# Which engine takes the third of the probabilities' low halves: DVE (before) or POOL (after)

## The reference, cut to what matters

```
h = tok(x)                                  # 16 images, 256 rows (tokens) of 256
h = h + attn(layernorm(h), Wq, bq, ...)     # 16 heads of 16, causal
h = h + ffn(layernorm(h), router, experts)  # 16 experts

attn: q, k, v = x Wq + bq, x Wk + bk, x Wv + bv
      scores  = (q k^T + mask) / sqrt(16)
      out     = softmax(scores) v           # for each image and head
```

## The kernel before, in words

| engine | steps at their places |
|---|---|
| PE | each place: the scores for the row maxima (lines 440 to 449), then the transposed scores for the exponential (463 to 472). 0, 1: product v. 3, 4, 6, 7, 9, 10, 0, 1: `times_v`. 3: transposes for xT (534), which wait for v_sum, since they use the same bank. 10: router product (525) |
| ACT | each place: exp n, n = (place + 2) mod 12, and then the rounding of probs n - 1. 2: negmax_hi. 3: first part of v (667). 4: xT_hi (649). 6: second part of v, hn2T. 8, 10: q_hi, k_hi. 11: router hidden |
| POOL | each place but 1, 4, 7, 10: low half n, n = (place + 1) mod 12. 4: v_rest (273) and the sum into hacc (280). 7: last part of v (276). 8: two times rstd (239, 241), for LN1 and LN2 |
| DVE | each place: the reduce to the row maximum (709, 713). 2, 5, 8, 11: `outputs`, then low half n = place (878). 2: v_sum (891). 5: xT_lo (863). 9: q_lo, second step of LN2 (756). 11: k_lo, then the normalised rows hn2 (769, two instructions). 1: hn1 (769, two instructions) |

## Time and profile before

### The profile page before, as it was taken

The page is one execution under the profiler, slowest core; times in us unless marked ns, Lnnn a source line. Parts: engine busy times, 40 slices in busy tenths (PEclk is TensorE's granted clock), DMA queues, the critical chain, the costliest instruction groups (busy, mean ns, idle before and its releaser), DMA issues.

```text
span 1197.5 us, 18952 instructions
## 1 busy us (share of the span) xinstructions
PE 939.6 (78%) x6870; PEld 806.0 (67%) x6870; DVE 734.1 (61%) x1598; ACT 575.2 (48%) x1065; POOL 678.9 (57%) x582
## 2 busy tenths in 40 slices
PE   0002147988888888877539999999999999999996
PEld 0002136767766776755318888888888888888885
DVE  6988846788888888875555345344444434544441
ACT  0000012777777877878414445444544544454442
POOL 2486041566656665656333567656656765665654
PEclk9999568899999999998759999999999999999999
DMA  8211749788688768811313545545445454555433
GB/s 209 90 54 67 158 124 141 122 127 136 130 143 134 131 126 146 137 42 37 125 55 69 107 112 86 109 110 119 97 107 114 85 106 112 109 106 108 83 53 36
DMA packets 105949, 127.59 MB, mean 107 GB/s; under 512 B 12288, under 2 KB 92160, under 8 KB 104832
## 3 DMA queue, kind: packets, MB, share of 16 engines
q1 hardware_dynamic: 81280, 92.81, 36.1%
q0 software_dynamic: 24576, 33.57, 17.2%
HBM read 79.67 MB, written 46.14 MB: 105 GB/s over the span
## 4 chain that ended last, share of the span: by engine, by line
PE 48%; DVE 2%; POOL 1%; issue 1%; ACT 0%; DMA 0%; POOLq 0%; ACTq 0%
PE y_ps L1120 15%; PE gate_ps L1106 15%; PE value_ps L1106 15%; PE xT_ps L1087 2%; DVE top_index L1260 1%; DVE top L1254 1%; DVE work L1262 0%; PE gate_ps L1129 0%; POOL out L1062 0%; POOL x_rows L1051 0%; DMA x_rows<-normed_scratch,slot_row 0%; ACT L1188 0%; ACT router_hidden L1188 0%; ACT xg_hi L1153 0%; DVE L L1252 0%
## 5 line engine op out<-in xcount | busy, mean ns | idle before, releaser
L1062 POOL DMA_INDIRECT out<-y_rows,slot_row x128 | 203.3, 1588 | 189.3 <-ACT y_rows L1166 159.9
L1229 DVE TENSOR_TENSOR hidden<-silu_g,value_ps 128x512 f32<-128x512 f32 x128 | 88.0, 688 | 306.5 <-PE value_ps L1106 171.5
L248 POOL TENSOR_TENSOR probs_k<-probs_full,probs_k 128x512 f16<-128x512 f32 x128 | 157.4, 1231 | 133.9 <-ACT probs_k L622 130.0
L1174 ACT ACTIVATE silu_g<-gate_ps 128x512 f32<-128x512 f32 x128 | 76.6, 598 | 276.7 <-PE gate_ps L1106 276.7
L1051 POOL DMA_INDIRECT x_rows<-normed_scratch,slot_row x128 | 149.6, 1169 | 56.4 <-issue 38.7
L615 ACT ACTIVATE probs_full<-scoresT_ps,log 128x512 f32<-128x512 f32 x192 | 132.4, 690 | 89.0 <-PE scoresT_ps L465 45.9
L1120 PE MATMUL y_ps<-w_hi,hidden_lo 128*128 128x256 f32 x512 | 144.9, 283 | 0.0
L1120 PE MATMUL y_ps<-w_lo,hidden_hi 128*128 128x256 f32 x512 | 144.9, 283 | 0.0
L1120 PE MATMUL y_ps<-w_hi,hidden_hi 128*128 128x256 f32 x512 | 144.7, 283 | 0.0
L622 ACT ACTIVATE probs_k<-probs_full 128x512 f16<-128x512 f32 x192 | 120.3, 627 | 0.0
L1106 PE MATMUL gate_ps<-xg_hi,w_hi 128*128 128x512 f32 x256 | 103.5, 404 | 2.1 <-ACT xg_hi L1153 2.1
(11 more groups left out here) (201 smaller groups left out, 2329.1 us busy)
## 6 DMA issues: line engine op xcount, KB each, us to landing
w_raw<-in_L_ffn_w SPq DMA_DIRECT2D x48, 512.0 KB, 4.1
q_stack<-q_scratch SPq DMA_DIRECT2D x96, 128.0 KB, 5.0
k_stack<-k_scratch SPq DMA_DIRECT2D x96, 128.0 KB, 8.2
x_tile<-in_x SPq DMA_DIRECT2D x4, 1024.0 KB, 5.1
h_scratch<-x_tile SPq DMA_DIRECT2D x4, 1024.0 KB, 3.9
hacc<-h_scratch SPq DMA_DIRECT2D x4, 1024.0 KB, 6.8
q_scratch<-q_hi SPq DMA_DIRECT2D x16, 256.0 KB, 2.2
q_scratch<-q_lo SPq DMA_DIRECT2D x16, 256.0 KB, 2.5
```

Of the source, the lines that this page charges most:

```text
L248: G.tensor_tensor(probs(b, 1, n), pf[N % 3][:].rearrange("p (a q) -> p a q", a=4 if n % 3 == 2 else 2), probs(b, 0, n), ALU.subtract).then ...
L1062: G.indirect_dma_start(out=rows, out_offset=bass.IndirectOffsetOnAxis(ap=idx[:, col:col + 1], axis=0), in_=ys[c][:, j, :], in_offset=None, ...
L1174: A.activation(sg[ft % 2][:], GP[ft % 2][:], ACT.Silu).then_inc(silu_done, 1)
L1229: V.tensor_tensor(hf[ft % 2][:], sg[ft % 2][:], VP[ft % 2][:], ALU.mult).then_inc(hf_done, 1)
```

## The change

The early return for n % 3 == 2 goes from POOL's `probs_lo`, so that POOL takes all twelve low halves of an image, each at the place of the rounding: the four of remainder 2 are now issued at places 1, 4, 7 and 10 (low half 2, 5, 8 and 11), first in their tick. They still count on the semaphore `pc_done`. DVE's four instructions, which stood one place later, go. No buffer, wait or DMA changes otherwise.

```diff
             def probs_lo(b, n):
                 N = NB * b + n
-                if n % 3 == 2:
-                    return
                 g.wait_ge(pa_done, N + 1)
                 G.tensor_tensor(probs(b, 1, n), pf[N % 3][:].rearrange("p (a q) -> p a q", a=4 if n % 3 == 2 else 2),
-                                probs(b, 0, n), ALU.subtract).then_inc(pb_done, 1)
+                                probs(b, 0, n), ALU.subtract).then_inc(pc_done if n % 3 == 2 else pb_done, 1)
...
                     if b >= 0 and r % 3 == 0:
                         outputs(b, r // 3)
-                    b, r = due(t, EX + 2)
-                    if b >= 0 and r % 3 == 2:
-                        v.wait_ge(pa_done, NB * b + r + 1)
-                        V.tensor_tensor(probs(b, 1, r), pf[2][:].rearrange("p (a q) -> p a q", a=4), probs(b, 0, r),
-                                        ALU.subtract).then_inc(pc_done, 1)
                     b, r = due(t, QP + 3)
```

## The result

The changed kernel takes 1187.3 us (median of 7 runs, 1184.6 to 1190.9), the kernel before 1195.0 on the same chip (7 runs, 1190.8 to 1199.7). The ratio is 0.9929, with a 95% interval of 0.9901 to 0.9957: faster by 0.7%, some 8 us. The profiled execution of after took 1186.07 us, of it 1184.3 span.

What follows compares the result with a forecast made beforehand. A ring of waits through DVE, PE, ACT and POOL was taken to set the attention round. From the 1195.5 us median, 5.4 gained over nine images and 0.8 lost in the tail gave 1190.9 us; range 1186 to 1200.

Steps and rivals of the forecast that it cites:

- The ring: Attention rounds: a loop of waits through DVE, PE, ACT and POOL sets their length; 24.03 us falls to 23.43.
- the pair: DVE's two L769 instructions for hn2, asked at z+3.32: end at z+4.02 after POOL's low half 0, instead of z+5.51.
- z: Moment DVE begins LN2's second step at place 9, from which times count; next one forecast at z+23.43 instead of z+24.02.
- The list of signs: Trace features that would show the forecast right (nine rounds of about 23.4 us) or wrong (rounds of 24 us).
- The size: Steady attention rounds: a gain of 0.60 us an image, 5.4 us for nine images.
- the upper bound of 1.0: Steady rounds: largest gain an image, if POOL's wait for probs 8 and 0.1 of ACT's spacing vanish.
- a sign against me: A long wait of ACT for POOL at exp 1 to 5 would show the forecast wrong; none was counted.
- The port rival: DVE and POOL exclude each other, so the round stays 24.03 us; time 1196.3 us, chance 0.27.
- The queue rival: POOL's low halves between places 4 and 8 stretch to 1.45 us; round 24.88, time 1204.0 us, chance 0.18.
- The tail and the ends: After the last scores: +0.15 us for each of two images and +0.5 at the very end, sum +0.8.
- The step that I had priced at +0.5: Very end of the tail: the last low half stands behind low half 10 instead of beside it, 0.5 us lost.
- The two rounds behind the nine: Images between 481 and 543 us: no change taken, within 1 us either way.

Runs made afterwards that it cites:

- experiment 1: Only low half 11 moved to POOL, against the kernel before: 1188.7 us, ratio 0.9932.
- experiment 2: Only low half 2 moved to POOL, against the kernel before: 1190.0 us, ratio 0.9945.
- experiment 3: Only low half 5 moved to POOL, against the kernel before: 1194.9 us, ratio 0.9983.
- experiment 8: Against the kernel with low halves 2, 5 and 11 moved, 8 on DVE: POOL does both rstd ahead of low half 9; 1181.0 us.
- experiment 9: Full change with the two rstd on POOL swapped, LN2's ahead of LN1's: 1186.5 us, ratio 0.9907 to the kernel before.
- experiment 10: Kernel with low halves 2, 5 and 11 moved, 8 on DVE, plus the two rstd swapped on POOL: 1179.5 us, ratio 0.9853.
- experiment 5: Full change without low half 8, which stays on DVE (2, 5 and 11 on POOL): 1180.6 us, ratio 0.986 to the kernel before.
- experiment 6: Full change plus one unread full-width POOL sum a round at place 5: 1197.0 us, ratio 0.9993 to the kernel before.
- second pair of profiles: The kernel before and the full change each profiled again, with no edit: 1197.1 and 1188.3 us.
- experiment 4: Only low half 8 moved to POOL, against the kernel before: 1216.6 us, ratio 1.0163.

## Why the prediction was right, and where not

**The ring.** It was there, and the way from low half 11 to the pair, to v_sum and to exp 6 went as worked out: the pair ended at z+4.03 (predicted 4.02), the reduce of place 2 at 6.66 (6.75), v_sum ended at 8.49 (8.61), low half 5 started at 11.31 (11.60), low half 9 at 19.56 (20.05), the next z at 22.93 (23.43). Experiments 1 to 3 price its parts one by one. (The list of signs has the pair "about 0.7" behind POOL's low half; the working has 0.47, and it was 0.48.)

**The size.** This is the term that was mis-sized: 0.60 us a round were forecast, 1.05 measured (9.42 over nine), just over the upper bound of 1.0, and with it the forecast of 1190.9 stood 3.6 us above the median that came. There are two causes of one kind, a wait that was read wrongly. I took a spacing without its wait as start to start less the idle time in the row. But idle time is counted from the end of the record before, and where ACT doesn't wait its next record starts about 0.1 before that end (the first part of v at 421.25 is 0.64 long, and exp 6 starts at 421.79). Exp 4 to exp 5 is 1.37 where I had 2.00 - 0.53 = 1.47, and first part of v to exp 6 is 0.54 where I had 0.94 - 0.28 = 0.66; with the 0.07 by which exp 4 came earlier this makes the 0.29 by which low half 5 did. And hacc to low half 6, 1.38 in the earlier trace rows, held a short wait for probs 6 that no bracket shows (in ACT's timeline of before that rounding ends at 434.87, 0.08 ahead of low half 6); with POOL busy it is 1.25.

**What closes the ring.** Here the prediction had the right number for a reason that was half wrong. It closed the ring through DVE: rstd, then z, then DVE's places 9 to 2 with the pair asking at z+3.3. Experiments 8 to 10 show that an earlier z alone shortens nothing, with low half 8 on POOL or without: POOL's own queue with ACT's steps behind it (exp 1, probs 0, router hidden) is on the path, up to PE's product v. The row that shows it is one that I had named as a sign against me and counted at none: ACT's wait of 1.06 for POOL at exp 1. It was there before the change, at 0.85, and the prediction overlooked it:
```profile
421.71 0.69 ACT L615 ACTIVATE probs_full<-scoresT_ps,log 128x512 f32<-128x512 f32 x1 [0.85 <-POOL probs_k L248]
```
Both ways start at the same low half 9 and meet at product v, at z+2.73 before and after, so the sum could not tell them apart, and that it held was luck in this point; experiment 8, which was to shorten the way through DVE, lengthened the one through POOL and ACT. No run shortens the way through POOL and ACT alone.

**The port rival** was wrong on the change and right on the mechanism. Where the pair asks while a low half runs on POOL, it ends 0.47 or 0.48 after it, in the full change and in experiments 1, 5, 8, 9 and 10, as the pair of the earlier trace rows did. In three of these seven (the full change, 1 and 5) it asked only 0.27 to 0.30 before the low half's end and was 0.75 to 0.77 long, hardly more than the 0.72 of the pair of place 1 (417.17 in the full change), so these three show little of a wait. The other four asked 0.81 to 1.16 before that end and were 1.28 to 1.63 long. In the kernel before the pair asked just after low half 0, at 424.48, and lost its second half to low half 1. The Trainium skill says in SBUF — State Buffer (section SBUF: two separate sides) that the port is held for a whole instruction: those four ends agree. The Trainium skill's page Perfetto Trace Analysis (section Optimizing Scalar/DVE Operations) warns that moving work between the two engines might not help for that reason; here the ratio of 0.9929 speaks against it, since the one collision that costs (1.63 instead of 0.75) went away with the move.

**The queue rival** did not come: 192 low halves average 1.17 us. But experiment 6 shows that it would have decided, at 0.71 a round for one more instruction of 1.05 us. What was missing was the stretch itself.

**The tail and the ends.** I took +0.8 and the sign was wrong: two images of the tail are 0.04 and 0.11 shorter (0.01 and 0.06 in the second pair of profiles), and the last round is 11.35 instead of 11.90. The step that I had priced at +0.5 is there (from the last rstd to the image sum 4.96 instead of 4.50), but the part ahead of it became 1.01 shorter (6.39 instead of 7.40). The two rounds behind the nine (from 481 us on in the kernel before) gained 0.8 and 1.4 in the first pair of profiles, 0.5 and 1.1 in the second, where I had taken none, within 1 us either way.

**What stays open.** By profiles the change gains 11 us (1197.5 and 1195.2 against 1184.3 and 1186.5), by the ratio 5 to 12. The rounds alone give 9.4, the tail and the end more; so the fill ahead of 265 us may give something back, but it scatters by 4 us in the kernel before, and two profiles of each do not settle it.

## What to carry to other kernels

In a pipeline that repeats exactly while every engine has idle time, ask of an instruction where it stands in the ring, not how long it is: one low half on the slower engine was worth 0.85 us a round at one place, 0.23 at another and cost 1.12 at a third. Try such moves one by one before all at once; here three of four are better than four. When a sum comes out right by one path, look for a second one of the same length, and shorten the first alone to see which of them counts.

## What the runs showed of the hardware

The granted clock can turn a longer ring into a still longer one. Where the steady rounds came with a clock of 1.00, they took 25.15 in experiment 4 and 23.65 in experiment 6 (23.87 once); in seven of nine rounds of the one and two of nine of the other a stretch at 0.50, some 3 to 7 us long, came behind a pause of PE of 1.4 to 1.9 us, and these rounds were 0.5 to 2.0 us longer. Two rounds of experiment 4 with pauses of 1.84 and 1.85 kept 1.00. In the kernel before, the full change and experiments 5 and 8 the windows of the steady rounds read 1.00.

Each DVE instruction of the pair takes 0.40 us alone. One that asks while a POOL low half runs waits it out: in experiments 8 and 9 the first of the pair was 1.31 and 1.29 long, and the pair was done 0.47 behind the low half. The POOL instruction that begins in that time takes 1.15 to 1.29 us, against the usual 1.16. In the kernel before the pair asks just after low half 0, low half 1 begins between its two halves, and the second half is 1.30 long.
